# Row loads, gathers and one-hot rows of the first tiles moved later in a fused conditional residual kernel

## The reference, cut to what matters

```python
# x (2, 2048, 512); cond_512 (2, 256); cond_64 (2, 64); fside (2, 32); three index arrays (2, 2048)
U = (mu @ W_dec + b_dec).reshape(B, 512 + 1, 30)        # W_dec (256, 513 * 30), mu = cond_512
param = einsum('bik,kj->bij', U, V)                     # V (30, 512)
x = x + (x @ param[:, :-1] + param[:, -1])
h = _ln(_ln(x, pw_g[path], pw_b[path]), cp_g[comp], cp_b[comp])
t = _ln(x, tm_g[comp], tm_b[comp])
m, n, r = (x + _mlp_ln(state)[:, None, :] for state in (cond_512, cond_64, fside))
s = _ln(x, ms_g[scale], ms_b[scale])
cat = concatenate([w0 * h, w1 * t, w2 * m, w3 * n, w4 * r, w5 * s])   # w = softmax(aw)
x = x + _mlp_ln(cat, int_W1, int_b1, int_W2, int_b2, int_g, int_be)   # silu(cat @ W1 + b1) @ W2 + b2, then _ln
```

## Time and profile before

| | |
|---|---|
| median of 3 runs | 637.97 us (635.06 to 638.03) |
| the profiled execution | 637.78 us |
| its span, instructions | 636.0 us, 9140 |
| busy PE, DVE, POOL, ACT | 93%, 64%, 61%, 32% of the span |
| DMA | 102.07 MB, 160 GB/s over the span |
| HBM read, written | 93.10 MB, 8.39 MB |

### The profile page before, as it was taken

How to read it: one execution, slowest core, us unless ns; L and a number is a source line. 1 busy time by engine, 2 the same in 40 slices (tenths; PEclk the granted TensorE clock), 3 DMA queues, 4 the chain that set the end, 5 groups by cost and what they waited for, 6 DMA issues and landing times.

```text
span 636.0 us, 9140 instructions
## 1 busy us (share of the span) xinstructions
PE 593.4 (93%) x2924; PEld 453.1 (71%) x2924; DVE 407.6 (64%) x749; ACT 204.9 (32%) x346; POOL 389.3 (61%) x499
## 2 busy tenths in 40 slices
PE   0899788989999999999999999999999999999995
PEld 0464245567878888888888777777888888787784
DVE  3411157658888888888865566556666565766655
ACT  3333235232333433334323323222333223323222
POOL 1013226666888888888856666676676676765820
PEclk9999799999999999999999999999999999999998
DMA  8999957513555445445524434444534344444301
GB/s 291 404 403 366 384 194 256 155 54 102 169 152 163 150 139 167 137 141 170 149 102 125 129 113 136 138 113 107 145 125 124 117 119 136 136 121 120 99 18 49
DMA packets 53119, 102.07 MB, mean 160 GB/s; under 512 B 10446, under 2 KB 23246, under 8 KB 52956
## 3 DMA queue, kind: packets, MB, share of 16 engines
q1 hardware_dynamic: 39872, 58.52, 27.0%
q0 software_dynamic: 12160, 42.04, 23.2%
q10 hardware_dynamic: 1052, 1.07, 0.5%
HBM read 93.10 MB, written 8.39 MB: 160 GB/s over the span
## 4 chain that ended last, share of the span: by engine, by line
PE 35%; POOL 16%; issue 12%; DVE 8%; DMA 8%; ACT 2%; POOLq 0%; DVEq 0%
PE bank L707 10%; PE bank L708 9%; PE bank L709 9%; DMA pwt<-in_pw,idx 7%; POOL h L1045 4%; PE bank L701 4%; POOL h L1043 3%; DVE bn L1215 3%; POOL rs L993 2%; POOL ctt L1010 2%; POOL ve L985 2%; POOL nm L998 1%; ACT ht L611 1%; DMA sgt<-in_ms_g,idx 1%; DVE x L1242 1%
## 5 line engine op out<-in xcount | busy, mean ns | idle before, releaser
L707 PE MATMUL bank<-W,ops 128*128 128x512 f32 x432 | 178.9, 414 | 1.3 <-DVE ops L1210 0.4
L708 PE MATMUL bank<-W,ops 128*128 128x512 f32 x432 | 171.3, 397 | 0.0
L709 PE MATMUL bank<-W,ops 128*128 128x512 f32 x432 | 171.0, 396 | 0.0
L707 PEld LDWEIGHTS bank<-W,ops 128*128 128x128 f32 x432 | 81.7, 189 | 29.7 <-issue 9.7
L555 ACT ACTIVATE ops<-bank 128x512 fp32r<-128x512 f32 x97 | 56.9, 589 | 136.8 <-PE bank L701 136.8
L709 PEld LDWEIGHTS bank<-W,ops 128*128 128x128 f32 x432 | 81.6, 189 | 20.0
L708 PEld LDWEIGHTS bank<-W,ops 128*128 128x128 f32 x432 | 81.9, 190 | 14.8
L1034 POOL TENSOR_TENSOR xop<-xraw,xop 128x512 fp32r<-128x512 f32 x32 | 41.8, 1307 | 65.9 <-ACT xop L526 65.8
L1210 DVE TENSOR_TENSOR ops<-bank,ops 128x512 fp32r<-128x512 f32 x97 | 66.2, 684 | 11.2 <-ACT ops L555 11.0
L1215 DVE BATCH_NORM_STATS2 bn<-h 128x6 f32<-128x512 f32 x32 | 22.2, 692 | 73.9 <-POOL h L1045 73.8
L985 POOL TENSOR_SCALAR ve<-mv 128x1 f32<-128x1 f32 x94 | 31.5, 336 | 39.5 <-DVE mv L1219 35.9
(11 more groups left out here) (143 smaller groups left out, 1058.4 us busy)
## 6 DMA issues: line engine op xcount, KB each, us to landing
ring<-in_W_dec SPq DMA_DIRECT2D x16, 960.0 KB, 12.1
xraw<-in_xT SPq DMA_DIRECT2D x32, 256.0 KB, 4.8
x<-in_x SPq DMA_DIRECT2D x32, 256.0 KB
out<-xb SPq DMA_DIRECT2D x31, 256.0 KB, 2.0
ring<-in_int_W SPq DMA_DIRECT2D x4, 1024.0 KB, 13.4
mnr<-in_int_W SPq DMA_DIRECT2D x12, 256.0 KB, 8.2
stash<-in_xT SPq DMA_DIRECT2D x12, 256.0 KB, 12.1
idxrep<-in_rows SPq DMA_DIRECT2D x64, 32.0 KB, 4.8
```

The source lines that it names most:

```text
L707: nc.tensor.matmul(bank[:, :], op[:, HI, c, :], w[:, HI, c, :], start=start and c == 0, stop=False)
L708: nc.tensor.matmul(bank[:, :], op[:, HI, c, :], w[:, LO, c, :], start=False, stop=False)
L709: last = nc.tensor.matmul(bank[:, :], op[:, LO, c, :], w[:, HI, c, :], start=False, stop=stop and c == KC - 1)
```

## The change

SP issues the rows of tiles 0 and 1 no longer before the items 13 to 15 of W_dec: those of tile 0 come behind item 15, those of tile 1 behind the T block, and those of tile 2 behind the H block instead of before it. POOL does the second half of the relayout before the gathers of tile 0. DVE makes the one-hot rows of tiles 0 and 1 no longer before the last `pre_low`, but behind the s rows of tile 0 and behind the first sum of tile 1.

```diff
                 if j == 2 * DECS - 3:
                     load_x(Tile(0))
-                    load_rows(Tile(0))
-                    load_rows(Tile(1))
                 if j >= SLOTS:
                     sp.wait_ge(dec_used, j - SLOTS + 1)
                 load_ring(sp, DEC[j])
+            load_rows(Tile(0))
             load_pre(NPRE - 2)
             sp.wait_ge(dec_used, slot[MLP1] + SLOTS + 1)
             load_ring(sp, MLP1)
             load_pre(NPRE - 1)
             load_ring(sp, BLK_T)
+            load_rows(Tile(1))
             sp.wait_ge(dec_used, 2 * DECS)
             load_ring(sp, MLP2[0])
             load_ring(sp, MLP2[1])
             load_x(Tile(1))
             load_ring(sp, MLP2[2])
             load_ring(sp, BLK_S)
-            load_rows(Tile(2))
             sp.wait_ge(mlp_used, 4)
             load_ring(sp, BLK_H)
+            load_rows(Tile(2))
             load_ring(sp, BLK_W2)
             load_x(Tile(2))
...
             to_features(pool, u_in_pool, 0, U_ROWS)
+            to_features(pool, u_in_pool, 1, U_ROWS[:KC])
             gathers(t0)
-            to_features(pool, u_in_pool, 1, U_ROWS[:KC])
             x_low(t0)
...
-            one_hot(Tile(0))
-            one_hot(Tile(1))
             pre_low(NPRE - 1)
...
             scale_rows(t0)
+            one_hot(t0)
             stacked(t1)
...
             first_sum(t1)
+            one_hot(t1)
             vec_norm()
```

## The result

| | before | the change |
|---|---|---|
| median | 638.03 us (11 runs, 635.06 to 639.28) | 632.56 us (11 runs, 629.54 to 635.72) |
| profiled execution, span | 637.78, 636.0 us | 633.35, 631.5 us |
| first product of tile 3's stack (PE line 768) | 145.22 us | 142.40 us |

The ratio is 0.9919 with a 95% interval of 0.9895 to 0.9943: the change makes the kernel 5.2 us faster (3.6 to 6.7). 632.0 was forecast.

The account below looks back on a forecast made before the run. DMA engines set the pace up to some 86 us, then TensorE. Item 15's 6.3 us gain, capped by tile 1's xT at 6.1, less 0.1 for small delays, gave 6.0: 632.0 us median, range 628.7 to 636.0.

Parts of the forecast that it names:

- Bytes ahead of item 15: W_dec's load: without rows (3.0 us) and gathers (3.3 us) in front, item 15 lands 6.3 us earlier, at 63.5.
- PE's start on the first layer: Small networks on PE: first layer starts when its weights land, at 68.2 instead of 75.11, 6.8 us ahead.
- almost 8: Lead in us of tile 0's chain after its embedding and stack, before later waits take part back.
- The cap: Tile 1's xT still lands at 82.9, limiting the lead to 6.1 us at tile 0's rstd.
- the clock in the new waits: Rival: PE's clock falls in waits of some 1.5 and 1.7 us from 80 to 85, costing about 2 us; chance 0.08.
- With gaps of under 1 us I take it to stay up: W_dec's last decodes: PE keeps full clock, a decode taking 1.01 us in place of 1.83.
- the prediction's own signs: Right: tile 0's transposes at 87 to 88.5, lead 6 at 160 us; wrong: clock 0.50 between 80 and 100.
- The rival's 634.0: Median time in us if PE's clock falls in the new waits before tile 1's embedding; chance 0.08.
- A microsecond by which PE's whole program runs earlier is worth a whole one: Where PE is never out of work, each microsecond of lead on entering that part shortens the kernel by one.
- Edits at nothing: Moving the two one-hots and tile 2's rows costs nothing; each one-hot would cost 0.25 us if PE waited.
- the slower rival: Tile 2's indices land late for POOL's gathers; at 110.9 us the kernel is 0.5% slower (641.2 us); chance 0.04.
- the change does not do what it says: Rival: gathers filled only gaps, slow stretch not the rows'; item 15 only 1.6 us earlier, 636.0 us; chance 0.12.

Follow-up runs that it names:

- before_again: The kernel before, unchanged, run once more with a profile: 638.77 us, ratio 0.9995.
- xt1_on_before: The kernel before with only tile 1's xT issued earlier, behind the last prefill tile's xT: 638.60 us, ratio 0.9992.
- gathers_xt1: The kernel before with tile 0's gathers behind the relayout and tile 1's xT issued early, row loads unmoved: 632.81 us, ratio 0.9912.
- xt1_rows1_late: The whole change with tile 1's xT issued early and tile 1's rows behind the second layer's second matrix: 629.65 us, ratio 0.9860.
- the filled kernels: The whole change with unread matmuls in PE's two new waits: 8 and 6 gave 634.22 us (0.9937), 6 and 4 gave 633.06 us (0.9931).
- small_undone: The whole change with tile 2's rows back before the H block and the one-hots at their old place: 633.65 us, ratio 0.9932.
- gathers_only: The kernel before with only tile 0's gathers moved behind the relayout: 632.49 us, ratio 0.9927.
- xt1_early: The whole change with tile 1's xT issued behind the last prefill tile's xT: 630.04 us, ratio 0.9882.

## Why the prediction was right, and where its steps were off

**Bytes ahead of item 15: right.** 3.0 us for the rows and 3.3 for the gathers were to bring the last decode from 69.82 to 63.5; it is at 63.52. Alone, the gathers are worth 3.8 (66.06), so the rows are worth 2.5, half a microsecond less than the 3.0 I took.

**PE's start on the first layer: right in kind.** 6.8 us ahead was forecast, 7.4 measured (67.67): its weights took 6.1 us instead of 12.0 and landed at 67.6, half a microsecond before my sum. The embedding of tile 0 is 7.3 us ahead (77.07), and its expansion 8.4 (79.14), since the stack's last step takes 0.28 us again: "almost 8" held.

**The cap: right in the change, half a microsecond later than assumed.** "Tile 1's xT lands when it did": 83.4 instead of 82.9. The lead at the rstd is 5.5 (85.44) in place of 6.1, at the embedding of tile 1 it is 4.4 in place of 5.0. Three experiments bear it out: with only the gathers moved, the last decode is 2.5 us later and the time no worse; moving the transfer is worth 2.9 us behind the change; and it is worth nothing on the kernel before. Two don't: with only the rows moved, Ust is the later cap and xT hardly waited for, and behind the gathers alone an early xT gained nothing.

**The step that was off: the clock in the new waits.** "With gaps of under 1 us I take it to stay up" was right for the decodes, but I gave the fall in the new waits a chance of only 0.08, because a wait of 1.90 us had left the clock alone. It fell in both profiles of the change. At half clock the embedding of tile 1 takes 1.23 us (0.74 before), and the transposes are 4.85 us ahead instead of 6.1; 0.6 of the missing 1.25 is the later xT, and with the waits filled the transposes come 0.6 to 0.7 sooner. A second fall near 104 takes another microsecond, and at tile 3 the lead is 2.8 (142.40). The forecast there was 6. By the prediction's own signs it was wrong here: the transposes at 88.99 and not by 88.5, a lead of 2.8 at 160 us, a clock of 0.50 between 80 and 100. The Trainium skill (TensorE: Matmul & The Clock Gate, "Part 1: The HAM clock gate (the "warmup" mystery)"), cited in the prediction, says that an idle TensorE goes to half clock, and the trace agrees (0.50 from 84 to 90 us). The rival's 634.0, which is 633.8 for a profiled run, is nearer to the profiled execution (633.35) than the forecast's 631.8; my 632.0 is nearer to the median.

What I overlooked is that one profile is no evidence here. The same wait of 1.89 or 1.90 us ahead of tile 0's first transposes stands in five profiles, with the same work on both sides and one wait of 1.08 or 1.09 us some 6 us before it. The clock stayed up in one, the one that I had, and fell in four: `before_again` (from 95 us), `xt1_on_before`, `gathers_xt1` and `xt1_rows1_late`. The kernel before pays for such falls, too.

**The total came out right partly by luck.** In the two first profiles, 2.8 us of lead at tile 3 and a rest that was 1.7 us shorter (489.1 against 490.8) make the 4.5 of the spans. But the first profile of the kernel before is an early one: tile 3 at 145.22, where `before_again` has 147.72 and `xt1_on_before`, whose time is the same, 147.90. The mean of the three less the change's 142.40 and 142.33 is 4.6 us, near the measured 5.2. So the forecast took a kernel before without the fall behind the wait at 93.84 and a change without the fall at 84, and as far as these profiles show the two largely cancel. "A microsecond by which PE's whole program runs earlier is worth a whole one" holds only to about 2 us either way: the filled kernels lost about 2 us of lead again behind tile 3.

**Edits at nothing: right** within 1.5 us. POOL's gathers of tile 2 (103.91) still wait for DVE's ht, not for their indices; the slower rival did not come. That the change does not do what it says is refuted by the 63.52.

## What to carry to other kernels

Where the DMA engines are full, moving transfers back does not make the later ones land sooner (tile 1's xT: 82.9 before, 83.4 now): it brings forward only what they were in front of. Sum the bytes up to each transfer that the path needs next; the first whose place in that sum is unchanged can be the cap, if nothing else comes later (here one transfer of 256 KB, 2.9 us for one line on top of the change's 5.2). When a stage gets ahead, look also at its new waits, since TensorE can pay for them again in its clock, and take more than one profile of the kernel before: here the start of tile 3's product lay 2.5 us apart in two.

## What the runs showed of the hardware

The scatter of one program goes with TensorE's clock: over the 23 executions of the change the mean granted clock runs from 0.984 to 0.999 and the time from 638.3 to 629.5 us, with a correlation of 0.83 between time and clock lost. That is a relation and not a cause: kernels whose clock was kept up by added matmuls (0.995 in the mean, the change 0.990) were not faster.

Short waits can be enough for the clock to fall. Behind a wait of 1.89 or 1.90 us, with steady work on both sides and one of 1.08 or 1.09 us some 6 us before, it fell in four of five profiles; behind single waits of 1.68 to 2.04 us ahead of tile 0's third transposes in five of thirteen profiles (both profiles of the change, `small_undone`, `gathers_only`, `xt1_early`); behind the two waits of 2.11 and 1.60 us with 1.06 us of work between them in both profiles. What decides in the single case was not found: 1.68 us was enough in one kernel and 2.04 us not in another.

Rows of x and indices are dear transfers: the 0.66 MB for two tiles cost 2.5 us at the last decode, the difference of `gathers_only` and the change, where 0.66 MB at 402 GB/s are 1.6. Which of them is dear was not tested apart.
